# Layer 0's attention on one core: the order of tiles on four engines

## The chip, the cores and the metric

One core of a Trainium2 chip runs the whole program. The metric is the device time of one execution in microseconds. Work in the core is done by five engines that run their own instruction lists in order and wait for each other through semaphores: TensorE (PE, with its weight loads listed as PEld), VectorE (DVE), ScalarE (ACT), GpSimd (POOL) and SyncE (SP), which here only issues DMAs.

## The reference, cut to what matters

The program computes two transformer layers for an input of 2 x 1024 x 128. Only the attention of layer 0 is touched by the change:

```python
B, S, H0, D = 2, 1024, 16, 128          # head size 8
q, k, v = x @ Wq.T + bq, x @ Wk.T + bk, x @ Wv.T + bv     # split into 16 heads of 8
scores = einsum('bhqd,bhkd->bhqk', q, k) / sqrt(8)
scores = where(tril, scores, -9e15)
out = einsum('bhqk,bhkd->bhqd', softmax(scores), v)       # then out @ Wo.T + bo
```

There are 2 x 16 = 32 heads (batch and head together), each with a causal 1024 x 1024 score matrix. The mixture of experts behind it, the attention of layer 1 and its trees of experts are the same in both kernels.

## The kernel before

`attend_layer0` works off the 32 heads. A head's scores are computed twice. First as **row tiles** (queries on the 128 partitions): tile i of 8 holds queries i x 128 to i x 128 + 127 and (i + 1) x 128 keys; it is cut at 512 columns, which makes 12 units numbered 0 to 11 (`UNITS`: 0 to 3 are row blocks 0 to 3 with 128, 256, 384 and 512 columns; 4, 6, 8 and 10 are the first 512 columns of blocks 4 to 7; 5, 7, 9 and 11 the remaining 128, 256, 384 and 512). PE computes a unit (`row_unit`, L401, and a mask matmul L404 on the diagonal block) into one of two PSUM banks, `ps_row`, and VectorE takes the maximum of each row (L551). From the maxima VectorE computes a shift per query in three bf16 parts (`shifts`, L557 to L563), PE turns them (`turn_shift`, L428) and ScalarE writes them as three more rows into q (L534), so that the second computation has the maximum subtracted already.

Then as **column tiles** (keys on the partitions): tile j of 8 holds keys j x 128 on and the 1024 - j x 128 queries that see them, so tile 0 is the widest (1024 columns) and tile 7 the narrowest (128). PE computes it (`column`, L419) into one of two PSUM buffers, `ps_col`, ScalarE takes the exponential (L530) into `prob`, and POOL zeroes the diagonal block's upper part (`hide`, L367). The turned shift uses the same two buffers as a ninth unit.

The products with v (`pv`, L445): for each of the tiles 0 to 7, 32 columns of v (8 values and a one for the sum) are the weights, and the 32-column results of four products lie beside one another on the partitions of `ps_out`, each in its own quarter of PE's columns. They come in three groups of four: x = 0, tiles 0 to 3 on the right 512 queries; x = 1, tiles 0 to 3 on the left 512; x = 2, tiles 4 to 7 on the right, added to the first. Within each of the last two groups the products have 512, 384, 256 and 128 columns. ScalarE copies `ps_out` to `oT` (L540), PE turns it in eight transposes (`turn_out`, L457) into the two banks of `ps_row`, VectorE adds the four quarters (L572), takes the reciprocal of the sum and multiplies (`keep`, L575 and L578).

The work of the heads overlaps in **sections**. Section n holds column tiles of head n, row units 4 to 11 of head n + 1 and 0 to 3 of head n + 2, the products of head n - 1, and transposes and division of head n - 2. The order on each engine is written out by hand in its `section`: PE L483 to L509, ScalarE L523 to L540, VectorE L582 to L594, POOL L370 to L385. Sections -1 to 3 and 28 to 33 are unrolled, 4 to 27 run in a loop of four. `row_unit` waits until VectorE has read the unit two before it (L400), `column` until ScalarE has read the one two before (L414); `col_unit`, `shift_unit` and `row_base` compute the semaphore counts of the order. POOL's `clear` (L356) zeroes the shift rows of q again before SP's next loads of q and k (L330, L331; four heads of buffers) are used.

PE's order in a section: column 0; turn_out twice; rows 4, 5; products x = 0; rows 6, 7; column 1; rows 8, 9; column 2; products x = 1; rows 10, 11; columns 3, 4; products x = 2; column 5; turn_shift; rows 0, 1; column 6; row 2; column 7; row 3. ScalarE: exponentials 0 to 5, the shift's copy, exponentials 6 and 7, the copy of `ps_out`.

Of the kernel before, what the change touches and what calls it, by code (L numbers as in the profile page):

```python
# [8 lines left out]
ALU = mybir.AluOpType  # L9
# [235 lines left out]
def attend_layer0(nc, g):  # L245
# [3 lines left out]
    with ExitStack() as ctx:  # L249
# [39 lines left out]
        TURN = 6  # L289
# [11 lines left out]
        def col_unit(n, j):  # L301

            return n * CU + 1 + j + (1 if j >= TURN and not is_at(n, NH - 1) else 0)

        def shift_unit(n):

            return n * CU - CU + 1 + TURN if not is_at(n, 0) else 0
# [17 lines left out]
        with nc.Block() as block:  # L325
# [17 lines left out]
            def _(pool):  # L343
# [17 lines left out]
                def hide(n, p, j, done):  # L361

                    pool.wait_ge(col_read, col_unit(n, j) + 1)
                    pool.sem_inc(calm, 1)  # L364
                    pool.wait_ge(calm, done)
                    diagonal = prob[:, p, PO[j]:PO[j] + P]
                    pool.affine_select(diagonal, diagonal, [[1, P]], ALU.is_ge, zero, base=0,  # L367
                                       channel_multiplier=-1).then_inc(hidden, 1)

                def section(n, i4, h):  # L370
# [6 lines left out]
                    if here:  # L377
                        values(n, h % 2)
                        done += 1
                        for j in range(TB):  # L380
                            done += 1
                            hide(n, h % 2, j, done)
# [8 lines left out]
            def _(pe):  # L391
                def row_unit(n, i4, h, unit, u):
# [4 lines left out]
                    if u == 0:  # L397
                        pe.wait_ge(qk_in[h], i4 * 32 + 32)
                        wait(pe, cleared, i4 * NQ + (h - NQ + 1))
                    wait(pe, row_read, unit - 1)  # L400
                    last = pe.matmul(ps_row[:, u % 2, 0:width], q[:, h, i * P:(i + 1) * P],  # L401
                                     k[:, h, c * CH:c * CH + width], start=True, stop=True)
                    if diag:
                        last = pe.matmul(ps_row[:, u % 2, width - P:width], g.identb[:, :], g.maskq[:, :],  # L404
# [3 lines left out]
                def column(n, p, h, j):  # L408

                    unit = col_unit(n, j)  # L410
                    if is_at(n, 0) and j == 0:
                        pe.wait_ge(col_read, 1)
                    else:
                        wait(pe, col_read, unit - 1)  # L414
                    buf = ((p + 1) % 2 + (unit - n * CU - 1)) % 2
# [7 lines left out]
                def turn_shift(n, p):  # L423

                    wait(pe, col_read, shift_unit(n) - 1)
                    pe.wait_ge(shift_ready, n + 1)
                    for i in range(TB):
                        m = pe.matmul(ps_col[0:NSH, p, i * P:(i + 1) * P], shift[:, p, i, :], g.identb[:, :],  # L428
                                      start=True, stop=True)
                    m.then_inc(col_ready, 1)  # L430

                def pv(n, p, x):


                    bank = 0 if x == 1 else 1
                    if x == 0:
                        pe.wait_ge(v_ready, n + 1)
                        wait(pe, out_read, n)
                        pe.wait_ge(col_read, col_unit(n, GR - 1) + 1)
                    else:  # L440
                        pe.wait_ge(hidden, n * TB + x * GR)
                    for a in range(GR):
                        j = a if x < 2 else a + GR
                        lo, hi = max(j * P, bank * CH), (bank + 1) * CH
                        m = pe.matmul(ps_out[a * GW:(a + 1) * GW, lo:hi], v[:, p, j, :],  # L445
                                      prob[:, p, PO[j] + lo - j * P:PO[j] + hi - j * P],
                                      start=(x < 2), stop=True, skip_group_check=True)
                    if x == 2:
                        m.then_inc(pv_done, 1)

                def turn_out(n, unit):

                    pe.wait_ge(out_read, n + 1)
                    for x in range(2):
                        pe.wait_ge(row_read, unit + (x - 1))
                        for i in range(4):
                            m = pe.transpose(ps_row[:, x, i * P:(i + 1) * P],  # L457
                                             oT[:, (4 * x + i) * P:(4 * x + i + 1) * P], g.ident[:, :])
                        m.then_inc(row_ready, 1)

                def section(n, i4, h):
                    here, after, late, next1, next2 = parts_of(n)
                    p = h % 2
                    base = row_base(n)
                    first = base + (2 if late else 0)

                    def rows1(u):
                        if next1:
                            row_unit(n + 1, i4 + (h + 1) // NQ, (h + 1) % NQ, first + (u - EARLY), u)

                    def rows2(u):
                        if next2:
                            row_unit(n + 2, i4 + (h + 2) // NQ, (h + 2) % NQ, first + (NU - EARLY) + u, u)
# [5 lines left out]
                    def weigh(x):  # L479
                        if after:  # L480
                            pv(n - 1, 1 - p, x)
# [8 lines left out]
                    rows1(7)  # L490
                    col(1)
                    rows1(8)
                    rows1(9)
                    col(2)
                    weigh(1)
                    rows1(10)
                    rows1(11)
                    col(3)
                    col(4)
                    weigh(2)  # L500
                    col(5)
                    if next1:
                        turn_shift(n + 1, 1 - p)
                    rows2(0)
                    rows2(1)
                    col(6)
                    rows2(2)
                    col(7)
# [5 lines left out]
                for u in range(EARLY):  # L514
                    row_unit(0, 0, 0, u, u)
# [3 lines left out]
            def _(act):  # L519
                def section(n, i4, h):  # L520
                    here, after, late, next1, _ = parts_of(n)
                    p = h % 2
                    for j in range(TB):  # L523
                        if here:
                            unit = col_unit(n, j)
                            buf = ((p + 1) % 2 + (unit - n * CU - 1)) % 2
                            act.wait_ge(col_ready, unit + 1)
                            if j == 0:
                                wait(act, pv_done, n - 1)
                            act.activation(prob[:, p, PO[j]:PO[j] + S - j * P], ps_col[:, buf, 0:S - j * P],  # L530
                                           ACT.Exp, scale=SCALE).then_inc(col_read, 1)
                        if j == TURN - 1 and next1:
                            act.wait_ge(col_ready, shift_unit(n + 1) + 1)
                            act.activation(q[SHIFT0:SHIFT0 + NSH, (h + 1) % NQ, :], ps_col[0:NSH, 1 - p, :],  # L534
                                           ACT.Copy).then_inc(col_read, 1)
                    if after:
                        act.wait_ge(pv_done, n)
                        if late:
                            act.wait_ge(row_ready, row_base(n) + 2)
                        act.activation(oT[:, :], ps_out[:, :], ACT.Copy).then_inc(out_read, 1)  # L540

# [3 lines left out]
            def _(dve):  # L545
                def reduce_rows(u, unit):
# [3 lines left out]
                    dve.wait_ge(row_ready, unit + 1)  # L550
                    dve.tensor_reduce(top[:, i, c:c + 1], ps_row[:, u % 2, 0:width], AX.X, ALU.max).then_inc(row_read, 1)  # L551

                def shifts(n, p, end):

                    chain = Chain(dve, step, n * STEPS)
                    dve.wait_ge(row_read, end)
                    chain(dve.tensor_tensor(peak[:, :], top[:, :, 0], top[:, :, 1], ALU.max))  # L557
                    wait(dve, col_ready, n * CU - 2 * CU - (CU - TURN - 2))
                    chain(dve.tensor_scalar(shift[:, p, :, 0], peak[:, :], -1.0, None, ALU.mult))
                    chain(dve.scalar_tensor_tensor(left[:, :], peak[:, :], -1.0, shift[:, p, :, 0], ALU.mult,  # L560
                                                   ALU.subtract))
                    chain(dve.tensor_copy(shift[:, p, :, 1], left[:, :]))
                    dve.tensor_tensor(shift[:, p, :, 2], left[:, :], shift[:, p, :, 1],  # L563
                                      ALU.subtract).then_inc(shift_ready, 1)

                def keep(n, base):

                    wait(dve, kept, n)
                    for x in range(2):
                        dve.wait_ge(row_ready, base + (x + 1))  # L570
                        grouped = ps_row[:, x, :].rearrange("p (i a w) -> p i w a", a=GR, w=GW)[:, :, 0:VW0, :]
                        dve.tensor_reduce(osum[:, 4 * x:4 * x + 4, :], grouped, AX.X, ALU.add).then_inc(row_read, 1)  # L572
                    dve.wait_ge(row_read, base + 2)
                    chain = Chain(dve, rec_ready, n)
                    chain(dve.reciprocal(rec[:, :], osum[:, :, DH0]))  # L575
# [1668 lines left out]
```

## Time and profile before

| | us |
|---|---|
| time, median of 3 runs | 2189.01 (2188.62 to 2190.98) |
| profiled execution | 2186.17 |
| its span, first to last instruction | 2184.5 |
| mean granted TensorE clock | 0.932 |
| busy PE / DVE / ACT / POOL | 1811.3 / 1506.7 / 1328.4 / 615.3 |
| layer 0's attention, first row unit to last division | 80.9 to 488.2 |

In the profile, a line of the timeline gives start and length in us, the engine, the source line, the operation, the tile written and the tile read, the shape, how many like instructions were merged, and in brackets how long the engine had stood idle and who ended that. A matmul's record reaches from its start to its modelled end and overlaps the next one's; so the distance between starts tells more than the sum of the lengths. A mean granted clock of 1.00 in a stretch is the 2.4 GHz level, 0.50 the 1.2 GHz level.

### The profile page before, as it was taken

The numbers are of one execution on the slowest core, as the hardware profiler recorded it, in microseconds if no ns is written. First come the engines' busy times: TensorE is split into PE (matmuls) and PEld (weight loads), VectorE is DVE, ScalarE is ACT, GpSimd is POOL, SyncE is SP. The second block draws the span as 40 slices with busy tenths as digits, with TensorE's granted clock in tenths as the row PEclk, the third lists the DMA queues.
The fourth block names the chain that finished last, engine by engine and source line by source line (L and its number), as shares of the span: only waits on it lengthen the run. The fifth ranks groups of instructions, "written<-read, shape, count | busy, mean of one in ns | idle before, by whom it ended". The sixth has DMA issues, their size and how long they took to land. (4 is left out here: it accounts for less than half of the span.)

```text
span 2184.5 us, 35939 instructions
## 1 busy us (share of the span) xinstructions
PE 1811.3 (83%) x10130; PEld 1041.6 (48%) x10163; DVE 1506.7 (69%) x4721; ACT 1328.4 (61%) x2819; POOL 615.3 (28%) x1540
## 2 busy tenths in 40 slices
PE   5688888889999789688886688888888956888887
PEld 3333333337777544345553355555555534555545
DVE  4566666642111355667773899999999978999985
ACT  3255555553444143223334799999999956999983
POOL 0133333310000125200001444444444432444440
PEclk8699999999999589889998799999999988999988
DMA  6200000001000112100002011111100010110000
GB/s 178 61 19 15 14 18 14 18 8 32 1 0 0 48 54 92 49 1 0 0 0 61 11 30 30 30 29 29 29 27 18 30 30 15 30 29 29 21 6 25
DMA packets 38186, 61.77 MB, mean 28 GB/s; under 512 B 10225, under 2 KB 15347, under 8 KB 38004
## 3 DMA queue, kind: packets, MB, share of 16 engines
q1 hardware_dynamic: 38069, 60.51, 9.2%
q8 instruction: 36, 0.59, 0.1%
q14 instruction: 81, 0.66, 0.1%
HBM read 34.14 MB, written 17.83 MB: 24 GB/s over the span
## 5 line engine op out<-in xcount | busy, mean ns | idle before, releaser
L1571 ACT ACTIVATE a_trash<-a_sc,a_search 128x1024 bf16<-128x1024 f32 (+7 forms) x768 | 586.1, 767 | 71.6 <-POOL a_search L1510 30.8
L1326 PE MATMUL a_ps_s<-a_k,a_q 128*128 128x512 f32 (+3 forms) x768 | 310.9, 520 | 64.9 <-DVE a_sc L1787 52.0
L1360 PE MATMUL a_ps_o<-a_kT,a_v 128*65 128x512 f32 (+3 forms) x768 | 288.2, 499 | 51.4 <-ACT a_kT L1588 49.6
L551 DVE TENSOR_REDUCE a_top<-a_ps_row 128x1 f32<-128x512 f32 (+3 forms) x384 | 199.2, 553 | 79.4 <-PE a_ps_row L401 39.2
L530 ACT ACTIVATE a_prob<-a_ps_col 128x1024 f32<-128x1024 f32 (+7 forms) x256 | 160.4, 651 | 149.0 <-PE a_ps_col L419 148.1
L1344 PE MATMUL a_ps_t<-g_ident,a_sc 128*128 128x128 f32 x1152 | 228.1, 284 | 20.2 <-ACT a_kT L1588 19.0
L1787 DVE TENSOR_SCALAR_CACHE_REDUCE a_sc<-a_ps_s,g_search 128x1024 f32<-128x1024 f32 (+7 forms) x256 | 207.9, 812 | 23.4 <-PE a_ps_s L1328 16.1
L1747 DVE SCALAR_TENSOR_TENSOR a_below<-a_sc,a_found 128x768 f32<-128x768 f32 (+7 forms) x256 | 211.3, 835 | 1.1
L1346 PE MATMUL a_ps_t<-a_minus,a_short 128*128 128x128 bf16 x1152 | 211.5, 221 | 0.0
L1326 PEld LDWEIGHTS a_ps_s<-a_k,a_q 128*128 128x128 f32 x768 | 132.4, 196 | 159.9 <-issue 100.3
L1344 PEld LDWEIGHTS a_ps_t<-g_ident,a_sc 128*128 128x128 f32 x1152 | 164.4, 143 | 90.7 <-ACT a_kT L1588 47.5
L1588 ACT ACTIVATE a_kT<-a_ps_t 128x512 f32<-128x512 f32 x288 | 161.9, 582 | 25.3 <-PE a_ps_t L1346 18.3
L1360 PEld LDWEIGHTS a_ps_o<-a_kT,a_v 128*65 128x65 f32 x768 | 89.1, 140 | 161.9 <-ACT a_kT L1588 101.2
L683 ACT ACTIVATE ex_hid<-ex_ps_h,le_b 128x512 f32<-128x512 f32 x128 | 87.5, 687 | 128.1 <-PE ex_ps_h L660 127.8
L1760 DVE MAX8 a_best<-a_below 128x8 f32<-128x160 f32 (+5 forms) x576 | 157.3, 329 | 1.1
L1571 ACT ACTIVATION_READ_ACCUMULATOR a_trash<-a_sc,a_search 128x1 f32 x768 | 147.9, 193 | 0.0
L367 POOL TENSOR_SCALAR_AFFINE_SELECT a_prob<-a_prob 128x128 f32<-128x128 f32 x256 | 73.3, 292 | 247.0 <-POOLq L364 246.9
L1581 ACT ACTIVATE a_short<-a_sc,a_cutoff 128x128 bf16<-128x128 f32 (+2 forms) x192 | 110.8, 656 | 43.5 <-DVE a_cutoff L1807 43.5
L734 DVE SCALAR_TENSOR_TENSOR l_acc<-ex_ps_y,l_comb,l_acc 128x128 f32 x112 | 31.9, 345 | 151.4 <-PE ex_ps_y L651 151.1
L1346 PEld LDWEIGHTS a_ps_t<-a_minus,a_short 128*128 128x128 bf16 x1152 | 123.5, 107 | 19.4 <-issue 19.4
L651 PEld LDWEIGHTS ex_ps_y<-le_w,ex_hid 128*128 128x128 f32 x1024 | 118.7, 192 | 13.4 <-issue 13.4
L401 PE MATMUL a_ps_row<-a_k,a_q 128*128 128x512 bf16 (+3 forms) x354 | 103.4, 336 | 20.8 <-DVE a_top L551 14.6
(267 smaller groups left out, 3378.2 us busy)
## 6 DMA issues: line engine op xcount, KB each, us to landing
a_v<-g_v SPq DMA_DIRECT2D x32, 260.0 KB, 2.3
q1turned<-p_full SPq DMA_DIRECT2D x32, 256.0 KB, 2.0
a_q<-q1turned SPq DMA_DIRECT2D x32, 256.0 KB, 3.5
a_k<-k1turned SPq DMA_DIRECT2D x32, 256.0 KB, 3.9
stack<-p_parts SPq DMA_DIRECT2D x24, 256.0 KB, 3.8
a_q<-stack SPq DMA_DIRECT2D x32, 96.0 KB, 2.2
a_k<-stack SPq DMA_DIRECT2D x32, 96.0 KB, 2.2
le_w<-d_w SPq DMA_DIRECT2D x1, 2048.0 KB, 8.9
```

The costliest lines, as they stand in the source:

```text
L530: act.activation(prob[:, p, PO[j]:PO[j] + S - j * P], ps_col[:, buf, 0:S - j * P], ACT.Exp, scale=SCALE).then_inc(col_read, 1)
L551: dve.tensor_reduce(top[:, i, c:c + 1], ps_row[:, u % 2, 0:width], AX.X, ALU.max).then_inc(row_read, 1)
L651: m = pe.matmul(ps_y[:, e % 2, t, :], hid[:, e % 2, hc, t * P:(t + 1) * P], w2[:, e, hc, :], start=(hc == 0), stop=(hc == HC - 1))
L1326: pe.matmul(ps_s[:, j % 2, c:c + w], q[:, p, i * P:width], k[:, p, c:c + w], start=True, stop=True)
L1344: pe.matmul(out, columns(h, i)[:, c * P:(c + 1) * P], g.ident[:, :], is_transpose=True, start=True, stop=False)
L1346: m = pe.matmul(out, short[:, OFF[i] + c * P:OFF[i] + (c + 1) * P], minus[:, :], start=False, stop=True)
L1360: m = pe.matmul(ps_o[0:VW1, lo // HALF, (lo % HALF) * P:CH], v[:, p, c, :], kT[:, u % 2, a * P:b * P], start=(c == 0), stop=(c == LAST[lo ...
L1571: act.activation(trash[:, u % 2, 0:(i + 1) * P], columns(h, i), ACT.Sign, scale=-1.0, bias=trials[:, p, c, i:i + 1], accum_out=balance[:, ...
L1588: act.activation(kT[:, u % 2, :], ps_t[:, u % 2, :], ACT.Exp).then_inc(t_read, 1)
L1747: lane[i] = did(dve.scalar_tensor_tensor(lows(i), columns(hs, i), found[:, i:i + 1], columns(hs, i), ALU.is_le, ALU.mult))
L1760: did(dve.max(best[:, p, i, a, :], buf[:, a * w:(a + 1) * w]))
L1787: dve.tensor_scalar(columns(h + 1, i), ps_s[:, j % 2, 0:(i + 1) * P], shift.rearrange("p n i -> p (n i)"), None, ALU.subtract, ALU.max, ac ...
```

## The change

All operations stay, with their shapes and counts; PE gets one more wait in a section, that of column tile 0 for the shift's copy. What changes is the order in a section on each engine, and with it the numbering of the semaphores, which is now read from two lists:

```diff
+        ROWS = (11, 7, 4, 10, 13, 12, 6, 9, 8, 5, 0, 2, 1, 3)
+        COLS = (0, 3, 6, 4, 1, 2, 7, 5, 8)
+        TURN_OUT, TURN_SHIFT = NU, TB
...
+        def row_place(n, x):
+            _, _, late, next1, next2 = parts_of(n)
+            there = [y for y in ROWS if (late if y >= TURN_OUT else next2 if y < EARLY else next1)]
+            return there.index(x)
+        def row_count(n, x):
+            return row_base(n) + row_place(n, x) + 1
```

Numbers 12 and 13 in ROWS are the two halves of turn_out, 8 in COLS is the shift. On PE:

```diff
-                    col(0)
                     if late:
-                        turn_out(n - 2, base)
-                    rows1(4)
-                    rows1(5)
-                    weigh(0)
...
+                    rows1(11)
+                    if after:
+                        weigh_right(n - 1, 1 - p)
+                    rows1(7)
+                    rows1(4)
+                    col(0)
+                    rows1(10)
+                    col(3)
+                    if late:
+                        turn_out(n, 1)
+                    if late:
+                        turn_out(n, 0)
+                    col(6)
+                    rows1(6)
+                    col(4)
+                    rows1(9)
+                    col(1)
+                    rows1(8)
+                    col(2)
+                    rows1(5)
+                    if after:
+                        weigh_rest(n - 1, 1 - p)
+                    col(7)
+                    rows2(0)
+                    col(5)
+                    rows2(2)
+                    rows2(1)
+                    if next1:
+                        turn_shift(n, p)
+                    rows2(3)
```

The groups x = 1 and x = 2 of the products become one, and the later four go to the quarters in reverse:

```diff
+                def weigh_rest(n, p):
+                    pe.wait_ge(hidden, n * TB + TB)
+                    for j in range(GR):
+                        weigh(p, j, j, 0, True)
+                    for j in range(GR, TB):
+                        m = weigh(p, j, TB - 1 - j, 1, False)
+                    m.then_inc(pv_done, 1)
```

`weigh_right` is the old x = 0. ScalarE's order becomes exponentials 0, 3, 6, 4, 1, 2, 7, the copy of `ps_out`, exponential 5, the shift's copy. VectorE's becomes maxima 11, 7, 4, 10, the two sums of the turned output (the right one first), maxima 6, 9, 8, 5, the reciprocal (`shares`), `shifts`, maxima 0, 2, 1, the multiplication (`keep`), maximum 3. POOL's `hide` follows the order of COLS. turn_out in section n reads the copy that ScalarE made in section n - 1, before ScalarE makes the next in the middle of section n; `column` of tile 0 waits for the shift's copy at the end of the section before.

## Rows read from the trace of the kernel before

**Rows 1.** Timeline, ScalarE: first exponential of heads 0, 2, 30; last division

```profile
93.99 1.02 ACT L530 ACTIVATE a_prob<-a_ps_col 128x1024 f32<-128x1024 f32 x1 [0.42 <-PE a_ps_col L419]
...
113.03 1.02 ACT L540 ACTIVATE a_oT<-a_ps_out 128x1024 f32<-128x1024 f32 x1
113.94 1.03 ACT L530 ACTIVATE a_prob<-a_ps_col 128x1024 f32<-128x1024 f32 x1
...
458.15 1.03 ACT L530 ACTIVATE a_prob<-a_ps_col 128x1024 f32<-128x1024 f32 x1
...
487.95 0.23 DVE L578 TENSOR_TENSOR l_o<-a_osum,a_rec 128x64 f32<-128x64 f32 x1
```

**Rows 2.** Windows, one section: each engine's busy us, then granted clock

```profile
core 0: us, PE busy (x) PEld busy (x) DVE busy (x) ACT busy (x) POOL busy (x), PEclk, DMA share, GB/s
...
302.30:314.60 12.30, 10.41 (x72) 4.01 (x72) 8.03 (x22) 6.83 (x10) 4.43 (x10) 1.00 0.05 16
```

**Rows 3.** Timeline, PE, out of two sections

```profile
298.69 1.09 PE L457 MATMUL a_ps_row<-g_ident,a_oT 128*128 128x128 f32 x8 [0.57 <-ACT a_oT L540]
...
303.83 1.05 PE L445 MATMUL a_ps_out<-a_prob,a_v 128*32 128x512 f32 x8
304.81 0.60 PE L401 MATMUL a_ps_row<-a_k,a_q 128*128 128x512 bf16 x2
...
305.31 0.65 PE L419 MATMUL a_ps_col<-a_q,a_k 128*128 128x512 bf16 x3
305.89 1.04 PE L445 MATMUL a_ps_out<-a_prob,a_v 128*32 128x512 f32 x8
...
307.72 0.61 PE L428 MATMUL a_ps_col<-g_identb,a_shift 128*3 128x128 bf16 x8 [0.52 <-ACT a_prob L530]
308.26 0.23 PE L401 MATMUL a_ps_row<-a_k,a_q 128*128 128x128 bf16 x1
```

**Rows 4.** Waits in one section: waiter, releaser, total us, times, longest

```profile
ACT a_prob L530 <- PE a_ps_col L419: 4.8, 4, 3.2
PEld a_ps_row L401 <- DVE a_top L551: 3.2, 5, 1.1
...
PEld a_ps_row L457 <- DVE a_top L551: 1.1, 1, 1.1
```

**Rows 5.** Groups by shape, VectorE, one section: busy us, mean ns

```profile
L551 DVE TENSOR_REDUCE a_top<-a_ps_row 128x1 f32<-128x512 f32 x7 | 4.7, 689 | 1.6 <-PE a_ps_row L401 1.5
...
L551 DVE TENSOR_REDUCE a_top<-a_ps_row 128x1 f32<-128x128 f32 x2 | 0.6, 286 | 0.9 <-PE a_ps_row L404 0.9
```

**Rows 6.** Timeline, VectorE, the same section

```profile
300.79 0.23 DVE L578 TENSOR_TENSOR l_o<-a_osum,a_rec 128x64 f32 x1 [0.43 <-DVE a_rec L575]
...
305.24 1.29 DVE L551 TENSOR_REDUCE a_top<-a_ps_row 128x1 f32<-128x512 f32 x2 [0.80 <-PE a_ps_row L401]
306.56 0.17 DVE L557 TENSOR_TENSOR a_peak<-a_top 128x8 f32<-128x8 f32 x1
...
307.49 0.17 DVE L563 TENSOR_TENSOR a_shift<-a_left,a_shift 128x8 bf16<-128x8 f32 x1
```

**Rows 7.** Groups by shape, ScalarE, one section

```profile
L530 ACT ACTIVATE a_prob<-a_ps_col 128x1024 f32<-128x1024 f32 x1 | 1.0, 1033 | 0.0
...
L534 ACT ACTIVATE a_q<-a_ps_col 3x1024 bf16<-3x1024 f32 x1 | 1.0, 1011 | 0.6 <-PE a_ps_col L428 0.6
...
L530 ACT ACTIVATE a_prob<-a_ps_col 128x128 f32<-128x128 f32 x1 | 0.3, 277 | 0.0
```

**Rows 8.** Timeline, POOL: the clearing of the shift's rows

```profile
310.75 1.89 POOL L356 TENSOR_TENSOR a_q<-a_none 3x1024 bf16<-3x1024 bf16 x1 [0.27 <-POOLq L384]
```

**Rows 9.** Groups by shape, PE, the 50 ns from 304.00 us on

```profile
L445 PE MATMUL a_ps_out<-a_prob,a_v 128*32 128x512 f32 x1 | 0.6, 617 | 0.0
...
L445 PE MATMUL a_ps_out<-a_prob,a_v 128*32 128x128 f32 x2 | 0.4, 284 | 0.0
```

**Rows 10.** Timeline, PE, the products of the last section

```profile
481.34 3.73 PE L445 MATMUL a_ps_out<-a_prob,a_v 128*32 128x512 f32 x24
```

More of the change, by code:

```diff
@@ L299, in row_base, with col_place, col_count, col_buffer @@
             return (NH - 2) * (NU + 2) + NU + {NH - 1: 10, NH: 12, NH + 1: 14}[n]
[L301 to L307, printed above, removed]
+        def row_place(n, x):
[4 more added lines that the diff above has]
+            return row_base(n) + row_place(n, x) + 1
+        def col_place(n, x):
+            here, _, _, next1, _ = parts_of(n)
+            there = [y for y in COLS if (next1 if y == TURN_SHIFT else here)]
+            return there.index(x)
+        def col_count(n, x):
+            return (0 if is_at(n, -1) else n * CU + 1) + col_place(n, x) + 1
+        def col_buffer(n, p, x):
+            return 0 if is_at(n, -1) else (p + 1 + col_place(n, x)) % 2
         def sections(eng, section):
@@ L391, in _, with row_unit @@
             def _(pe):
-                def row_unit(n, i4, h, unit, u):
+                def row_unit(n, i4, h, count, bank, u, opens):
                     i, c = UNITS[u]
@@ L408, in column @@
                 def column(n, p, h, j):
[L410 to L415, printed above, removed]
+                    if j == COLS[0]:
+                        pe.wait_ge(col_read, 1 if is_at(n, 0) else col_count(n - 1, TURN_SHIFT))
+                    wait(pe, col_read, col_count(n, j) - 2)
+                    buf = col_buffer(n, p, j)
                     n_q = S - j * P
@@ L430, in turn_shift @@
                     m.then_inc(col_ready, 1)
[L432 to L459, printed above, removed]
+                def weigh(p, j, a, bank, first):
+                    lo, hi = max(j * P, bank * CH), (bank + 1) * CH
+                    return pe.matmul(ps_out[a * GW:(a + 1) * GW, lo:hi], v[:, p, j, :],
+                                     prob[:, p, PO[j] + lo - j * P:PO[j] + hi - j * P],
+                                     start=first, stop=True, skip_group_check=True)
@@ L545, in _, with reduce_unit @@
             def _(dve):
-                def reduce_rows(u, unit):
+                def reduce_unit(u, count, bank):
                     i, c = UNITS[u]
                     width = min(CH, (i + 1) * P - c * CH)
[L550 to L575, printed above, removed]
-                    b = n // H0
-                    o = g.o0[:, bass.ds(b, 1), :, bass.ds((n % H0) * DH0, DH0)]
-                    dve.tensor_tensor(o, osum[:, :, 0:DH0],
-                                      rec[:, :].rearrange("p (i o) -> p i o", o=1).broadcast_to([P, TB, DH0]),
-                                      ALU.mult).then_inc(kept, 1)
+                    dve.wait_ge(row_ready, count)
```

162 lines of the change are left out of this document (105 added, 57 removed).

## The prediction

> **What bounds the kernel now.** First the starts of the widest exponential of each head on ScalarE [rows 1]. Layer 0's attention handles 32 heads; head 0 starts at 93.99 us, head 2 at 113.94, head 30 at 458.15, and the last division ends at 488.2. The 28 sections between heads 2 and 30 take (458.15 - 113.94) / 28 = 12.29 us each; what lies before takes 19.95 us for two sections, and what lies behind 30.0 us.
>
> Then the busy time in one such section [rows 2]: PE 10.4 us of 12.3, DVE 8.0, ACT 6.8, POOL 4.4, at a granted clock of 1.00. No engine is full. PE's 10.4 is less full than it looks, since a matmul's record goes on after the next one has started; I count from start to start [rows 3]. Row tiles 10 and 11 (512, 512 and 128 columns) take 304.81 to 305.31 = 0.50 us, 0.43 ns a column; the 10240 bf16 columns of a head (4608 of rows, 1024 of masks, 4608 of column tiles) make 4.4 us. A group of four products takes 303.83 to 304.81 = 0.98 us, and some 0.09 us more passes before it (tiles 3 and 4, 1152 columns at 0.43, would be done in 0.49 of the 0.58 us from 305.31 to 305.89); of the 0.98 I count two 512-column records of 0.45 one after the other and 0.08 for the way out. The shift's eight small matmuls take 307.72 to 308.26 = 0.54, and I put the same 0.09 before them, where they don't wait.  Eight transposes take 1.0. So PE has 4.4 + 3 x 1.07 + 0.63 + 1.0 = 9.2 us of work and stands still for 3.1.
>
> The waits say where [rows 4]: ScalarE stands 4.8 us for column tiles, and PE's weight loads stand 3.2 us for VectorE's reads of the row tiles. The order causes both. Row tiles come in pairs, so both PSUM buffers fill together, VectorE reads them one after the other (about 0.6 us each), and PE, which takes its instructions in order, stands before the next pair with the column tile for ScalarE behind it. ScalarE's copy of a head's output, the transposes, eight row tiles, the shift and ScalarE's copy of the shift follow one another in a ring, and that ring is 12.3 us long.
>
> **The change, part by part.** No work is added; every instruction stays, in another order. I walk one section of the new order, with t = 0 at row tile 11 on PE. Prices: a reduction of 512 / 384 / 256 / 128 columns lasts 0.69 / 0.55 / 0.42 / 0.29 us (512 and 128 from [rows 5], the others lie between them), the next starts about 0.09 before its end (two in 1.29 us, [rows 6]); exponentials last from 1.03 (1024 columns) to 0.28 (128), 0.11 for each 128 columns, the shift copy 1.01 [rows 7], and the next starts 0.1 before the end (113.03 + 1.02 against 113.94, [rows 1]); from a matmul's start to its reader 0.43 us for 512 columns (304.81 to 305.24); from the end on VectorE to PE 0.06 (307.66 to 307.72) [rows 3, 6].
>
> - t = 0 row 11; right-hand products 0.36 to 1.35; row 7 at 1.35; row 4 at 1.55 (it waits 0.04 for row 11's reduction); column 0 at 1.77; row 10 at 2.22; column 3 at 2.44.
> - Transposes: 2.79 (waiting 0.07 for row 4's read) and 3.40 (0.11 for row 10's), to 3.89. In the kernel before they wait at the head of the section for ScalarE's copy (0.57 us of idle PE before 298.69, [rows 3]); now that copy lies in the middle of the section before, long done.
> - Column 6 3.89, row 6 4.00, column 4 4.22, row 9 4.46, column 1 4.68, row 8 5.17 (waits 0.11), column 2 5.40, row 5 5.72 to 5.84. On ScalarE the six exponentials run from 2.42 to 6.89 and wait 0.25 us in all: a narrow tile is read while PE fills the wide one behind it.
> - The eight products, 5.94 to 7.19. Before, two groups stood apart with 0.98 us each, and each lasts as long as its 512-column product. The new assignment puts 512 + 128 or 384 + 256 on each quarter of the columns, 640 on all. At 0.45 / 512 = 0.88 ns a column, 640 columns twice (a product leaves two records) take 1.13 us, with 0.04 for the second start and 0.08 for the way out 1.25. Against 2.14 with both ways in, PE saves 0.8 us. One look bears this out: at 304.0 us, 0.17 after the first start, two 128-column records overlap the same 50 ns as the first 512-column one [rows 9], so each quarter runs on by itself.
> - VectorE: row 5's reduction ends at 6.50, the chain of the shift (306.56 to 307.66 = 1.1 us, [rows 6]) at 7.62. The 0.43 us of idle VectorE before the multiplication [rows 6], an exposed address computation, now lies behind reductions.
> - Column 7 7.19, row 0 7.24, column 5 7.36, row 2 7.54, row 1 8.00 (waits 0.23 for row 0, whose reduction stood behind the chain), shift 8.26 to 8.80, row 3 8.80, next row 11 at 9.07. ScalarE: column 7 7.45, output copy 7.63 to 8.65, column 5 to 9.04, shift copy 8.94 to 9.95.
>
> The next column 0 comes at 10.84 and needs the shift copy at 10.01: 0.8 us to spare. POOL is busy 4.4 us of a section [rows 2], its longest step is the clearing of the shift rows, 1.89 [rows 8]; with an estimated 0.25 of sequencing around each of its ten steps it needs 6.9. Its order follows ScalarE's, and the mask of column 5, the last one, is done at about 0.6, five microseconds before the eight products want it. SP loads q and k a whole section early; its queue carries nothing else here. So the section is **9.07 us**, with PE at 8.5 of work and 0.6 of waits: PE's own order becomes the bound. I add 0.08 for what a walk leaves out: 9.15.
>
> Full sections: 28 x (12.29 - 9.15) = 88 us. Edges: heads 0 and 1, without transposes at first, are held by VectorE's row work, about 7.6 and 8.3 us against 9.3 and 10.6 in the 19.95: 4 us. Behind head 30: a section without early rows (about 8.2 instead of 12.1) and a tail that overlaps better but ends in the same serial copy, transposes and division at half clock: 8 us. Sum 88 + 12 = 100 us. The profiled execution has 2186.17 us (span 2184.5), the median of the three runs 2189.01; nothing else in the program changes, so 2189 - 100 = **2089 us**.
>
> **A rule against it.** By the rows a quarter does not wait for the others: the second 128-column record overlaps the first 512-column one [rows 9], and in the tail three groups run back to back, 24 records in 3.73 us, at a clock that is partly half [rows 10]. The Trainium skill, "TensorE: Matmul & The Clock Gate", Part 3, "What overlaps and what doesn't", says that matmuls start and end strictly in program order. By that rule the eight products would cost what rival 2 says; the trace disagrees so far.
>
> **Rivals.**
> 1. Hand-overs are dearer than walked. There are 14 row tiles, and with single tiles each has its own round trip PE, VectorE, PE; if every one is 0.06 to 0.1 us late, the section is 9.9 to 10.4 us. For it: both PE and VectorE (7.7 of work) are now near full, so a delay isn't absorbed. Against: the walk shows VectorE's buffer free before PE comes at 10 of 14 places. Time at 10.0: 28 x 2.29 + 10 = 74 us less, 2115.
> 2. The later four products don't run on by themselves but in order behind the whole of the first four. The second halves of the first four start at 0.45 us; the first halves of the later ones then start from 0.6 (after the 128-column one) to 0.9, their second halves from 1.06 on, and the 512-column one ends at 1.5; with the way out 1.6 instead of 1.25. Section 9.5, 28 x 0.35 = 10 us less gain: 2099.
> 3. Slower: products of one column quarter block the in-order engine, so that the eight run one after another. Their place is on PE's path. Price: 2560 columns twice at 0.88 ns and 0.2 for starts are 4.7 us, 3.45 more than walked. The section is then 12.5 us, and the right edge gains go too: 28 x 0.23 = 6 us more, 2195. It decides from about 4.5 us for the eight products on. Against: the overlap in [rows 9, 10].
> 4. The order isn't what holds the section: the copy of the shift, now last on ScalarE, gates the next column 0 and closes a ring as long as the old one. It would have to eat the 0.8 us of slack and 3.2 more: 2189.
>
> **How the numbers follow.** The forecast (section 8.8 to 9.5) 0.60, rival 1 0.25, rival 2 0.07, rival 3 0.04, rival 4 0.04. The forecast's own range is 2078 to 2099. Below: if PE's waits vanish, the section is 8.5 and the edges give 14, 2069; above, rival 1 up to a section of 10.2, 28 x 2.1 + 10 = 69, 2120. Range 2070 to 2120. A measurement tells about 0.2% (4.4 us) from no change. Faster 0.92 (forecast, rivals 1 and 2), same 0.04 (rival 4), slower 0.04 (rival 3).
>
> **What would show it.** Right: starts of the 1024-column exponential 9.0 to 9.4 us apart; the 16 records of the eight products within 1.4 us; ScalarE's wait for column tiles down from 4.8 to below 2; transposes without a wait for the output copy; granted clock 1.00. Wrong: a wait of column 0 for the shift copy; product records one after another; PE waits for row reads above 1.5 us a section (rival 1); a lower granted clock in the stage.

## The result and the profile after

| | before | after |
|---|---|---|
| median time, us | 2188.82 (2188.42 to 2190.98) | 2087.31 (2085.63 to 2088.20) |
| ratio, 95% interval | | 0.9538 (0.9524 to 0.9552) |
| profiled execution, its span | 2186.17, 2184.5 | 2088.2, 2086.5 |
| mean granted clock | 0.932 | 0.932 |
| start of head 0's exponential | 93.99 | 95.00 |
| heads 0 to 2 | 19.95 | 17.55 |
| a section, heads 2 to 30 | 12.29 | 9.02 |
| head 30 to the last division's end | 30.0 | 20.8 |
| from there to the end of the span | 1696.3 | 1700.6 |

The stage's frame comes from the timelines of ScalarE and VectorE, as in [rows 1]. Where two or three exponentials follow without a gap they share one line; the start is what counts.

```profile
95.00 1.90 ACT L549 ACTIVATE a_prob<-a_ps_col 128x1024 f32<-128x1024 f32 x3 [0.96 <-PE a_ps_col L436]
...
112.55 1.62 ACT L549 ACTIVATE a_prob<-a_ps_col 128x1024 f32<-128x1024 f32 x2 [1.37 <-PE a_ps_col L436]
...
365.19 1.62 ACT L549 ACTIVATE a_prob<-a_ps_col 128x1024 f32<-128x1024 f32 x2 [1.35 <-PE a_ps_col L436]
...
385.72 0.23 DVE L627 TENSOR_TENSOR l_o<-a_osum,a_rec 128x64 f32<-128x64 f32 x1
```

The 28 full sections take (365.19 - 112.55) / 28 = 9.02 us. From these starts and the end of the last division: head 0 comes 1.0 later, heads 0 to 2 give 2.4, the full sections 344.2 - 252.6 = 91.6, the tail 9.2, and 4.2 go in the rest of the program. Together 98.0 us, the difference of the two spans.

One section in the view by windows, as [rows 2], and its waits, as [rows 4] (waiter, releaser, total us, times, longest):

```profile
283.98:292.99 9.01, 8.82 (x72) 4.62 (x72) 7.71 (x22) 6.80 (x10) 4.49 (x11) 1.00 0.07 22
```

```profile
ACT a_prob L549 <- PE a_ps_col L436: 2.1, 3, 1.4
PEld a_ps_row L420 <- DVE a_top L585: 1.9, 4, 0.8
```

The instructions are as many, and as long, as before. PE's records now cover 8.82 of 9.01 us instead of 10.41 of 12.30. ScalarE's wait for column tiles fell from 4.8 to 2.1. The same section on PE's timeline, as [rows 3]:

```profile
284.40 1.26 PE L478 MATMUL a_ps_row<-g_ident,a_oT 128*128 128x128 f32 x8
285.49 0.27 PE L436 MATMUL a_ps_col<-a_q,a_k 128*128 128x256 bf16 x1
...
287.52 1.28 PE L452 MATMUL a_ps_out<-a_prob,a_v 128*32 128x512 f32 x16
288.74 0.23 PE L436 MATMUL a_ps_col<-a_q,a_k 128*128 128x128 bf16 x1
...
289.76 0.61 PE L445 MATMUL a_ps_col<-g_identb,a_shift 128*3 128x128 bf16 x8
290.53 0.22 PE L423 MATMUL a_ps_row<-g_maskq,g_identb 128*128 128x128 bf16 x1 [0.16 <-DVE a_top L585]
290.58 0.38 PE L420 MATMUL a_ps_row<-a_k,a_q 128*128 128x512 bf16 x1
...
290.95 1.06 PE L452 MATMUL a_ps_out<-a_prob,a_v 128*32 128x512 f32 x8
291.95 0.28 PE L420 MATMUL a_ps_row<-a_k,a_q 128*128 128x256 bf16 x1
...
292.36 0.59 PE L436 MATMUL a_ps_col<-a_q,a_k 128*128 128x512 bf16 x2
```

The transposes wait for no copy (their line has no releaser, where [rows 3] has 0.57 us for ACT). The 16 records of the eight products are over when column 7 starts: 288.74 - 287.52 = 1.22 us. VectorE in the same stretch:

```profile
286.02 2.07 DVE L585 TENSOR_REDUCE a_top<-a_ps_row 128x1 f32<-128x512 f32 x4
288.00 0.19 DVE L621 RECIPROCAL a_rec<-a_osum 128x8 f32<-128x8 f32 x1
288.12 0.17 DVE L599 TENSOR_TENSOR a_peak<-a_top 128x8 f32<-128x8 f32 x1
...
289.14 1.25 DVE L585 TENSOR_REDUCE a_top<-a_ps_row 128x1 f32<-128x128 f32 x3
290.31 0.21 DVE L627 TENSOR_TENSOR l_o<-a_osum,a_rec 128x64 f32 x1
```

The multiplication stands directly behind a maximum, without the 0.43 us of idle time that it had in [rows 6].

### The profile page after: what moved, and what is told of

Its sections match the earlier page's. It is cut to its first block and busy times, and to the rows that moved or that the text cites. A ratio compares the mean times of both kernels' runs of the same rounds, so it can differ in the third digit from the quotient of the medians.

```text
span 2086.5 us, 35986 instructions
## 1 busy us (share of the span) xinstructions
PE 1760.6 (84%) x10131; PEld 1056.3 (51%) x10163; DVE 1497.3 (72%) x4721; ACT 1327.3 (64%) x2819; POOL 619.0 (30%) x1540
## 5 line engine op out<-in xcount | busy, mean ns | idle before, releaser
L709 PE MATMUL ex_ps_y<-le_w,ex_hid 128*128 128x128 f32 x1024 | 118.8, 275 | 0.0
L420 PE MATMUL a_ps_row<-a_k,a_q 128*128 128x512 bf16 (+3 forms) x353 | 114.7, 335 | 4.8 <-DVE a_top L585 2.7
```

The source lines that it names most:

```text
L709: m = pe.matmul(ps_y[:, e % 2, t, :], hid[:, e % 2, hc, t * P:(t + 1) * P], w2[:, e, hc, :], start=(hc == 0), stop=(hc == HC - 1))
```

## The experiments

In the quoted expectations Theory 1 is the account that I held to, in most runs PE's order as the bound; the other theories and the rivals are named there. "Section" below is always the mean from head 2's widest exponential to head 30's. All times are medians, with their range; the kernel before had medians of 2186.9 to 2188.6 beside them.

### Are the quarters independent?

```diff
-                        m = weigh(p, j, TB - 1 - j, 1, False)
+                        m = weigh(p, j, j - GR, 1, False)
```

> The changed kernel with the later four of the eight products on the same column quarters as the first four (tile 4 with tile 0, 5 with 1, 6 with 2, 7 with 3), so one quarter carries 512 + 512 columns and another 128 + 128, instead of 640 on each. Theory 1 (PE's own order bounds the section of 9.03 us, and a quarter runs on by itself): the eight products take two more 512-column records less two of 128, 1.88 us instead of 1.22, and the section grows by 0.6 us to 9.65 (a little goes into PE's wait for row 0's reading); some 30 sections give 2087 + 18 = 2105 us. Theory 2 (matmuls start in program order across the quarters, so the assignment doesn't matter): the same time as the changed kernel, within 3 us of 2087. Theory 3 (VectorE's and ScalarE's hand-overs hold the section and absorb work on PE): also about 2087, but with the products seen to take 1.9 us.

Measured: 2106.56 us (2105.09 to 2108.64), ratio 0.9631 (0.9615 to 0.9647), section 9.61. PE's timeline:

```profile
290.07 1.90 PE L452 MATMUL a_ps_out<-a_prob,a_v 128*32 128x512 f32 x16
291.91 0.23 PE L436 MATMUL a_ps_col<-a_q,a_k 128*128 128x128 bf16 x1
```

The same eight products, in the same order in the program, take 1.84 us instead of 1.22 once the fullest quarter holds 1024 columns instead of 640. Two records for each of 384 more columns in 0.62 us are 0.81 ns a column and record, near the 0.88 of the forecast. The fullest quarter sets the time, and all of the 0.6 arrives in the section: PE's order is on the path here.

That a quarter runs on without waiting for the others is seen in the records that have begun in the first 0.67 us, by shape:

```profile
L452 PE MATMUL a_ps_out<-a_prob,a_v 128*32 128x512 f32 x2 | 1.0, 604 | 0.0
...
L452 PE MATMUL a_ps_out<-a_prob,a_v 128*32 128x128 f32 x4 | 0.6, 279 | 0.0
```

Tile 4's product (512 columns) stands ahead of tile 7's (128 columns) in the program. Yet both records of tile 7 have begun here, and neither of tile 4, whose quarter still works on tile 0's.

### Is the early copy what freed the transposes?

```diff
                     weights(7)
-                    if after:
-                        copy_out()
                     weights(5)
                     if next1:
                         keep_shift()
+                    if after:
+                        copy_out()
```

> The changed kernel with ScalarE's copy of the output moved from before exponential 5 to the end of the section, behind the shift's copy; all else as changed. Theory 1 (the old ring through this copy was a main part of the 12.3 us): the copy then ends at 10.8 us of the section's own time, and the next head's right-hand products, which overwrite the same PSUM, wait for it: they start at 10.9 instead of 9.4, the section is 10.5 us, 1.5 more, 30 times: 2087 + 44 = 2131 us. PE shows an idle time of about 1.5 us a section before the right-hand products, released by the copy. Theory 2 (PE's total work sets the section, and the place of the copy is of no weight, since the transposes read it a section later): 2087 within 3 us.

Measured: 2139.14 us (2138.35 to 2139.81), ratio 0.9779 (0.9762 to 0.9795), section 10.81 as a mean: ordinary ones 10.6, and three (those that end at heads 9, 22 and 27) of 12.2. PE's timeline in an ordinary one:

```profile
262.52 1.06 PE L452 MATMUL a_ps_out<-a_prob,a_v 128*32 128x512 f32 x8 [1.57 <-ACT a_oT L561]
```

The copy's place is worth 1.6 us in an ordinary section (expected: 1.5), of the 3.3 us between the two kernels. It doesn't come back at the transposes, which read a copy of the section before, but at the right-hand products: they overwrite `ps_out`, which the copy is still reading. PE stands 1.57 us there. The total is 8 us above Theory 1's 2131; the three longer sections are 4.8 of it, and why they are longer isn't settled.

### Single tiles or pairs

```diff
                     rows1(4)
-                    col(0)
                     rows1(10)
+                    col(0)
                     col(3)
...
                     col(6)
-                    rows1(6)
                     col(4)
+                    rows1(6)
```

and so on to the end of the section, with row tiles and column tiles in pairs on PE alone.

> The changed kernel with PE's row tiles and column tiles in pairs again (rows 4 and 10, columns 0 and 3, columns 6 and 4, rows 6 and 9, columns 1 and 2, rows 8 and 5, columns 7 and 5, rows 0 and 2); the orders of ScalarE, VectorE and POOL and the buffer numbers stay as changed. Theory 1 (single tiles between one another hide the round trips of both buffers): PE waits 0.4 us for row 7's reading before row 10, and 0.5 us for ScalarE before column 4, with the rest behind; section 10.0 us, 2087 + 29 = 2116 us. Theory 2 (the order of the numbers and the moved copies and transposes are what counts, not single or paired): 2087 to 2092 us.

Measured: 2121.28 us (2120.19 to 2122.77), ratio 0.9695 (0.9679 to 0.9711), section 10.08. Waits over ten sections, first of the kernel after, then of this one:

```profile
ACT a_prob L549 <- PE a_ps_col L436: 20.7, 27, 1.5
```

```profile
ACT a_prob L549 <- PE a_ps_col L436: 33.7, 40, 2.3
...
PEld a_ps_col L436 <- ACT a_prob L549: 10.4, 30, 0.5
```

Turn and turn about is worth 1.06 us a section. In pairs PE's loads stand for ScalarE's reads 30 times in ten sections, and then ScalarE stands for PE: each side waits for the other in turn. The total lies 5 us above Theory 1's 2116, since heads 0 to 2 take 21.4 us here instead of 17.6.

### The division in two halves

```diff
                         gather(0, False)
+                    if late:
+                        shares()
+                        keep()
                     reduce_rows(6)
...
                     reduce_rows(5)
-                    if late:
-                        shares()
...
                     reduce_rows(1)
-                    if late:
-                        keep()
```

> The changed kernel with VectorE's reciprocal and multiplication back in one piece right behind the two sums of the turned output, as in the kernel before. Theory 1: the 0.2 us reciprocal, 0.43 us of exposed address computation and 0.2 us multiplication lie before the maximum of row 6, which then starts 0.75 us later; row 8 on PE needs that bank and waits as much, and columns 2, 5 and the eight products queue behind it: section 9.7 us, 30 times 0.65, 2087 + 19 = 2106 us. Theory 2 (VectorE is busy 7.75 of 9.04 us and has room for it): 2087 to 2091 us.

Measured: 2109.21 us (2105.49 to 2110.79), ratio 0.9639 (0.9623 to 0.9655), section 9.76. VectorE's timeline:

```profile
290.53 0.20 DVE L621 RECIPROCAL a_rec<-a_osum 128x8 f32<-128x8 f32 x1
291.16 0.23 DVE L627 TENSOR_TENSOR l_o<-a_osum,a_rec 128x64 f32 x1 [0.43 <-DVE a_rec L621]
291.30 1.15 DVE L585 TENSOR_REDUCE a_top<-a_ps_row 128x1 f32<-128x512 f32 x2
```

The gap of 0.43 us before the multiplication is back, and the two operations hold up maximum 6 by 291.30 - 290.53 = 0.77 us. The section is longer by 0.74. That VectorE's delay reaches the end in nearly full size shows that VectorE is on the path here, not only PE.

### The shift ahead of the reciprocal

```diff
                     reduce_rows(5)
-                    if late:
-                        shares()
                     if next1:
                         shifts(n + 1, 1 - p)
+                    if late:
+                        shares()
```

> The changed kernel with VectorE's reciprocal moved from before the shift chain to behind it. In the changed kernel the reciprocal's 0.12 us (start to start) stand before the chain, row 0's maximum stands behind the chain, and PE waits for that before row 1. Theory 1: the chain, row 0's maximum and row 1 come 0.12 us earlier, the section is 8.90 us, and 30 of them save 3.5 us, 2083.5 us. Rival: the reciprocal then stands before row 0's maximum instead, which starts when it did; the section and the time stay, 2087 us.

Measured: 2088.90 us (2084.44 to 2093.25), ratio 0.9548 (0.9532 to 0.9564), section 9.07. No gain, and the rival expectation holds. In the kernel after the reciprocal (288.00) lies beneath the pause that the peak (288.12) makes behind maximum 5 anyway: from that maximum's start to the peak's it is 0.32 us with the reciprocal between and without it. Moved, it stands before maximum 0, which begins 0.20 us after the chain's last operation instead of 0.09.

### Parts of the change in the kernel before

The merged products alone, in the old order:

```diff
+                def pv_rest(n, p):
+                    pe.wait_ge(hidden, n * TB + TB)
+                    for j in range(TB):
+                        bank, a = (0, j) if j < GR else (1, TB - 1 - j)
...
-                        if after:
+                        if after and x == 0:
                             pv(n - 1, 1 - p, x)
+                        if after and x == 2:
+                            pv_rest(n - 1, 1 - p)
```

> The kernel before, with one part of the change alone: the product groups x = 1 and x = 2 merged at the place of x = 2, the later four on the quarters in reverse. Everything else in the old order. Theory 1 (the ring of waits through row tiles 10 and 11, shift chain and shift copy is what the section consists of, and PE's work counts only where it lies in the ring): row tile 10 no longer stands behind 0.98 us of products but only behind VectorE's reading, 0.78 us earlier; the shift comes 0.77 us earlier, the section takes 11.55 us instead of 12.33, and 30 of them give 2189 - 23 = 2166 us. Theory 2 (only the PE work saved counts): 0.8 us of work less but PE stands still for 3.1 us anyway, so about 2189 to 2185 us. Theory 3 (the merged products are most of the gain): the gain is half or more of the 102 us, below 2138 us.

Measured: 2166.89 us (2166.03 to 2168.88), ratio 0.9904 (0.9887 to 0.9921), section 11.54: 0.75 us a section, where the forecast took 0.8 off PE.

The transposes and the division later, in the old order:

```diff
                     col(0)
-                    if late:
-                        turn_out(n - 2, base)
...
                     col(1)
+                    if late:
+                        turn_out(n - 2, turned)
...
+                    if next1:
+                        for u in range(EARLY, 8):
+                            reduce_rows(u, base + (u - EARLY))
                     if late:
-                        keep(n - 2, base)
+                        keep(n - 2, base + (4 if next1 else 0))
```

> The kernel before, with the transposes of the output alone moved on PE from behind column 0 to behind column 1, and VectorE's sums and division with them behind the maxima of rows 4 to 7. Theory 1 (the ring through copy and transposes made the 12.33 us): rows 4 and 5 and the first products no longer wait for the copy and 1.1 us of transposes; row 10 and with it the shift come 0.9 us earlier, section 11.4 us, 30 times: 2189 - 27 = 2162 us. Theory 2 (the amount of waiting stays and only moves, because the copy is still at the end of the section): 2189 to 2184 us.

Measured: 2165.77 us (2164.75 to 2168.48), ratio 0.9899 (0.9884 to 0.9915), section 11.61, 0.68 less. Both edits in one kernel:

> The kernel before with the two parts that were tried alone, together: the groups x = 1 and x = 2 of the products merged at the place of x = 2 (alone: section 12.33 to 11.57 us), and the transposes of the output behind column 1 with sums and division behind the maxima of rows 4 to 7 (alone: 11.60). Theory 1 (a part is worth what it takes from the wait that ends last, and the two shorten the same wait, that before row 10): once the transposes are late, row 10 is held by row 8's maximum, which stands behind the division, so taking the products from before it gives only about 0.17 us more; section 11.4 us, total 2166 - 5 = 2161 us. Rival (the two gains add up): 12.33 - 0.75 - 0.73 = 10.85 us, 2189 - 44 = 2145 us.

Measured: 2158.89 us (2155.20 to 2161.09), ratio 0.9870 (0.9852 to 0.9888), section 11.36. Together 0.93, not 0.75 + 0.68 = 1.43. PE's timeline shows what comes in their place, the pair of row tiles 10 and 11:

```profile
312.52 0.85 PE L401 MATMUL a_ps_row<-a_k,a_q 128*128 128x512 bf16 x2 [0.77 <-DVE a_top L566]
```

Row 10 needs the buffer of row 8, whose maximum now stands behind the sums and the division; much of PE's saved time is waited away there, as Theory 1 said. That the pairs as such are the cause is argued. The remaining 11.36 - 9.02 = 2.3 us come with the new order as a whole and aren't divided further.

### Which engine is the bound now?

Three kernels with work left out: without the mask matmuls (PE, 1024 columns a head), with maxima over at most 256 columns (VectorE), and with both. These compute other scores. The last two have two executions each.

```diff
-                    if diag:
+                    if False:
                         last = pe.matmul(ps_row[:, bank, width - P:width], g.identb[:, :], g.maskq[:, :],
```

> The changed kernel without the eight mask matmuls on the diagonal blocks of the row tiles of each head. That leaves out the masking in the first computation of the scores, so the maximum of a query also sees up to 127 later keys; the softmax is shifted by a somewhat larger number. Theory 1 (PE bounds the section): 8 x 0.056 = 0.45 us less PE work a section; two of the waits grow by 0.05, so 8.65 instead of 9.03, 30 times: 2087 - 11 = 2076 us. Theory 3 (VectorE, whose 7.75 us of work stay, and the hand-overs hold it): PE only waits longer, 2087 to 2084 us.

```diff
-                    dve.tensor_reduce(top[:, i, c:c + 1], ps_row[:, bank, 0:width], AX.X, ALU.max).then_inc(row_read, 1)
+                    dve.tensor_reduce(top[:, i, c:c + 1], ps_row[:, bank, 0:min(width, 2 * P)], AX.X, ALU.max).then_inc(row_read, 1)
```

> The changed kernel with VectorE's maxima taken over at most the first 256 columns of a row tile instead of up to 512; the rest of each tile is left out of the maximum, so the shift is smaller than it should be. VectorE has 6 x 0.27 + 2 x 0.14 = 1.9 us less work a section. The total is not the measure here, because the numbers of layer 0 steer a branch in layer 1 (found in the run without masks: one more slow pass of 27 us); the section is, the distance of the 1024-column exponentials. Theory 1 (PE bounds it, VectorE only by the round trips): the waits for row reads but half of the one for row 0 vanish, 9.02 to 8.6 us. Theory 3 (VectorE is the bound since its maxima and chain follow one another): the section falls by most of 1.9 us, to 7.5 or less, below PE's work, which is impossible if that is 8.45. Theory 4 (neither: the ring over row 5, the shift chain and row 0 holds it): 8.9 or more.

> Both at once: maxima over at most 256 columns, and no mask matmuls (both parts of the first score computation are left out as told before). Without masks alone the section fell by 0.10 us only where PE had 0.45 less to do. Theory 1, amended (PE and VectorE's round trips are at their limits together, so taking from one alone is answered by a wait for the other): with both taken the full 0.45 shows beside what the short maxima give, 8.2 us. Theory 4: as in the other run, 8.8 or more.

| | time, us | ratio (95%) | section | behind the last division |
|---|---|---|---|---|
| after | 2087.31 | 0.9538 | 9.02 | 1700.6 |
| no masks | 2113.24 (2110.57 to 2116.33) | 0.9664 (0.9648 to 0.9681) | 8.92 | 1727.2 |
| short maxima | 2150.32 (2147.98 to 2152.66) | 0.9830 (0.9812 to 0.9848) | 8.73 | 1771.0 |
| both | 2145.15 (2144.07 to 2146.24) | 0.9807 (0.9789 to 0.9825) | 8.40 | 1776.7 |

Two neighbouring heads of each, ScalarE's timeline, in this order:

```profile
262.91 1.62 ACT L549 ACTIVATE a_prob<-a_ps_col 128x1024 f32<-128x1024 f32 x2 [1.33 <-PE a_ps_col L436]
271.95 1.62 ACT L549 ACTIVATE a_prob<-a_ps_col 128x1024 f32<-128x1024 f32 x2 [1.52 <-PE a_ps_col L436]
```

```profile
258.75 1.62 ACT L549 ACTIVATE a_prob<-a_ps_col 128x1024 f32<-128x1024 f32 x2 [1.33 <-PE a_ps_col L436]
267.54 1.62 ACT L549 ACTIVATE a_prob<-a_ps_col 128x1024 f32<-128x1024 f32 x2 [1.41 <-PE a_ps_col L436]
```

```profile
252.96 1.62 ACT L549 ACTIVATE a_prob<-a_ps_col 128x1024 f32<-128x1024 f32 x2 [1.05 <-PE a_ps_col L436]
261.42 1.90 ACT L549 ACTIVATE a_prob<-a_ps_col 128x1024 f32<-128x1024 f32 x3 [1.13 <-PE a_ps_col L436]
```

The three totals are above that of the kernel after although the sections are shorter. The time is lost in layer 1: VectorE's repeated search at L1731 runs only for heads where the data ask for it. By source line, in the kernel after, then without masks (count, shortest/median/longest ns, first and last start):

```profile
L1731 DVE MAX8 a_again<-a_sc x2: 295/562/828, 1683.3 to 1692.8; 128x8 f32<-128x128 f32 x1, 128x8 f32<-128x640 f32 x1
```

```profile
L1731 DVE MAX8 a_again<-a_sc x4: 295/428/828, 1677.9 to 1892.5; 128x8 f32<-128x128 f32 x2, 128x8 f32<-128x640 f32 x1, 128x8 f32<-128x384 f32 x1
```

The head that takes that branch in addition keeps ScalarE waiting for VectorE once, for 28.5 us:

```profile
ACT a_short L1639 <- DVE a_cutoff L1865: 28.5, 1, 28.5
```

The rest of the program is 27 us longer. With short maxima three heads take the branch instead of one, in the kernel with both left out as well, and the rest is 70 and 76 us longer. So these three kernels are to be compared by their sections alone; the expected total of 2076 without masks missed this.

By sections: the masks are worth 0.10 of the 0.45 us that their 1024 columns take on PE; short maxima, which take VectorE from 7.74 to 6.31 us of a section, are worth 0.29; both 0.62, more than 0.39. With VectorE's maxima short the masks count 0.33. Theory 1 alone had expected 8.65 without masks, and the 8.92 is nearer Theory 3, by which PE only waits longer; for short maxima it had 8.6 (8.73 came), and amended, for both, 8.2 (8.40 came). Neither engine alone is the bound: PE's order is, with VectorE's returns of the row buffers in it, and shortening one leaves the wait for the other. A VectorE bound, which would have let the section fall to 7.5 with short maxima, is excluded, and so is a bound by ScalarE's exponentials, since 8.40 was reached with these unchanged.

## Why the prediction was right, and where it was not

**The section.** Walked at 9.07, and taken as 9.15; it is 9.02. Starts after row tile 11, as walked and as measured (the first three from the row 11 at 290.58, the others from the one a section earlier, at 281.58): products 0.36 and 0.37, row 7 1.35 and 1.36, column 0 1.77 and 1.78, transposes 2.79 and 2.82, the second half 3.40 and 3.42, column 6 3.89 and 3.91, row 8 5.17 and 5.19. The rest was a little quicker than walked: row 1 comes at 7.91 instead of 8.00. The 0.08 added for what a walk leaves out wasn't there. One price had a doubtful source: the 0.06 us from VectorE's end to PE was read at the shift's matmuls, where [rows 3] names ScalarE as the releaser. In the kernel after it holds, since maximum 0 ends at 289.43 and row 1 starts at 289.49. 28 sections gave 91.6 instead of 88.

**The products.** 1.25 predicted, 1.22 measured, and the moved quarters gave 1.84. The step that rested on one overlap of 50 ns [rows 9] holds, and with it rivals 2 and 3 fall. The rule of the Trainium skill ("TensorE: Matmul & The Clock Gate", Part 3, "What overlaps and what doesn't") that matmuls start and end in program order is not what these column-tiled products do: with the quarters moved, tile 7's records begin before tile 4's. The 1.22 us alone would not show it. With the balanced quarters the later four begin in program order anyway (287.79, 287.99, 288.20 and 288.41), so a rule of starts in order costs nothing here, and the price of rival 2 that the prediction gave it doesn't follow.

**What bounds it.** "PE's own order becomes the bound" was half of it. The walk had 8.5 us of work and 0.6 of waits on PE. With VectorE's maxima short the section is 8.73, so the length of the maxima is worth 0.29. PE's records cover 89.9 of 90 us there (202 to 292), so its work is 8.7 at most; the walk's 8.5 is neither confirmed nor excluded by that. The masks' 0.45 us of PE work counted 0.10 while VectorE was in the way. The walk itself contained this, since it has VectorE's returns at each tile; the sentence drawn from it did not.

**The signs.** Starts of the widest exponential 9.02 apart, at the lower edge of 9.0 to 9.4; 16 records within 1.4; ScalarE's wait 2.1, where I had put below 2; transposes without a wait for the copy; clock 1.00 in the section. The sign against, PE's waits for row reads above 1.5 us, was badly made: weight loads waited 1.9 us for maxima, but mostly while the matmul before them was still running. PE's own records, whose ends are modelled, leave only 9.01 - 8.82 = 0.2 us uncovered.

**Rivals 1 and 4.** Dearer hand-overs would have given sections of 9.9 and more. A section of that length comes where PE works in pairs (10.08), but by the order, at the same prices. The ring through the shift's copy did not form: no wait of column tile 0 for it is in the section's waits. A ring through ScalarE's other copy does form if that copy goes last (10.6).

**The front.** Here the forecast failed: 4 us expected, 1.4 came. Sections 0 and 1 were to take 7.6 and 8.3 us by VectorE's row work; they took 8.79 and 8.76, and head 0 started 1.0 later. In head 0's section PE's loads wait for ScalarE's reads of the column buffers (total, times and longest), and column 6, the third tile, stands on PE:

```profile
PEld a_ps_col L436 <- ACT a_prob L549: 2.7, 5, 1.0
```

```profile
96.07 0.28 PE L436 MATMUL a_ps_col<-a_q,a_k 128*128 128x256 bf16 x1 [0.63 <-ACT a_prob L549]
```

The next section has 1.9 us of such waits of the loads; ten ordinary sections have 2.2 together. The term that failed is "held by VectorE's row work": without transposes and products between the column tiles, PE reaches the third tile while ScalarE still reads the first. The run with short maxima agrees: with 1.4 us less for VectorE to do in a section, the first two take 8.53 and 8.72 us, hardly less.

The later start comes from the order, which the forecast left out: column tile 0 now stands behind row tiles 11, 7 and 4, at a mean clock of 0.51 from 80 to 95 us. The first row unit and the first column tile on PE, in the kernel before, then after:

```profile
80.90 0.29 PE L401 MATMUL a_ps_row<-a_k,a_q 128*128 128x128 bf16 x1 [0.76 <-DMA a_k<-stack]
...
92.90 1.06 PE L419 MATMUL a_ps_col<-a_q,a_k 128*128 128x512 bf16 x2
```

```profile
81.02 0.29 PE L420 MATMUL a_ps_row<-a_k,a_q 128*128 128x128 bf16 x1 [0.69 <-DMA a_k<-stack]
...
94.11 0.84 PE L436 MATMUL a_ps_col<-a_q,a_k 128*128 128x512 bf16 x2
```

From one to the other it is 12.0 us, and in the three other kernels with the old order too. In the kernel after it is 13.1, as in the moved quarters, the late copy, the undivided division and the moved shift, and 13.5 where the pairs put row 10 ahead of column 0 as well.

**The tail** gave 9.2 for 8. **The rest of the program** is 4.2 us longer; other kernels that compute the same scores have 1696.7 to 1701.2 us there, so it moves by that much without a reason in the change. What makes it move stays open. Errors that offset one another bring the total so near, and that is luck: they are +3.6 in the sections, +1.2 in the tail, -2.6 at the front and -4.2 behind, and sum to -2.0: the profiled execution fell by 98 instead of 100, while the median fell from 2188.82 by 101.5 to 2087.31.

## What to carry to other kernels

Where two engines pass tiles through two buffers, let PE alternate between its two readers and walk one period with all hand-overs, tile by tile: it came out within 1% here (9.07 and 9.02 us), while the busy shares told only that nobody was full. Put a copy that frees a buffer as early as its data allow, and small dependent VectorE operations behind long ones that hide their gaps (0.74 us a section here). Walk the first sections as well, with what is missing in them.

## What the hardware showed that I had not expected

That column-tiled fp32 products run on independently in each quarter was a guess from one overlap; it held over 16 records, to 0.6 us when the balance was changed (1.22 and 1.84 us), and there even against the order of the program. Unexpected was how far two partial remedies in the old order fell short of their sum (0.93 for 0.75 + 0.68 us a section), and that leaving out masks in layer 0 lengthened layer 1 by 27 us through a branch on the data: a kernel with other values isn't to be judged by its total.
